# Weight loads, fp8 rounding and side jobs in other slots of an attention loop, and two head columns centred on VectorE

## What is computed

```python
x = x + tanh(g_xattn) * xattn(layernorm(x), ctx)     # 8 groups of heads
x = x + tanh(g_ffn) * ffn(layernorm(x))
# xattn
ln = ln(hidden) ; q = fp8_linear(ln, wq); k = fp8_linear(ln, wk); v = ...; qx = fp8_linear(ln, wqx)
kx, vx = split(einsum(cond, w_kv_x));   q, k, qx, kx are layer-normed per head of 128
core = gqa(q, k, v); xout = gqa(qx, kx, vx)          # softmax(q k^T / sqrt(d)) v
out = einsum(fp8(cat(core, xout) / smooth), wproj) * scales
# fp8_linear: fp8(clip(x / in_scale, -448, 448)) * in_scale, times wq, times a scale
# ffn: bitlinear(x, w): x rounded to int8 steps per token; w -> clip(round(w / mean|w|), -1, 1) * mean|w|
```

## Time and profile before

| | us |
|---|---|
| median of three runs | 1812.07 (1807.82 to 1817.33) |
| the profiled execution | 1815.84 |
| its span, first to last instruction | 1814.1 |
| preamble and ramp, up to the first exponential (slot 0) | 115.6 |
| slots 0 to 511 | 1372.1 |
| the tail behind them | 326 |

### The profile page before, as it was taken

One profiled execution on the slowest core, in us unless ns is written; L12 is line 12 of the kernel. 1 busy time (PEld: TensorE's weight loads), 2 busy tenths in 40 slices (PEclk: granted clock), 3 DMA queues, 4 the chain that ended last, 5 costly groups with the idle time before them and its releaser, 6 DMA issues.

```text
span 1814.1 us, 35237 instructions
## 1 busy us (share of the span) xinstructions
PE 1620.1 (89%) x11164; PEld 1005.9 (55%) x11164; DVE 1533.6 (85%) x3391; ACT 1371.8 (76%) x3439; POOL 1100.2 (61%) x1421
## 2 busy tenths in 40 slices
PE   2368899889999999999999898999999978999997
PEld 1345555555666665666566555666666633444443
DVE  7568889999897899989887999999988876777776
ACT  6458999879989998999998788899988872222222
POOL 3677888877887777787776666777767641000000
PEclk9689999999999999999999999999999999999999
DMA  3257888779999998999897989999998896243200
GB/s 104 90 151 164 186 194 190 178 169 230 230 244 196 218 226 191 205 217 250 193 216 169 224 192 200 222 229 225 251 222 169 184 246 216 70 112 87 76 24 18
DMA packets 669596, 325.48 MB, mean 179 GB/s; under 512 B 552288, under 2 KB 595424, under 8 KB 669152
## 3 DMA queue, kind: packets, MB, share of 16 engines
q1 hardware_dynamic: 669408, 323.17, 79.2%
HBM read 140.61 MB, written 48.23 MB: 104 GB/s over the span
## 4 chain that ended last, share of the span: by engine, by line
PE 45%; DVE 24%; ACT 12%; issue 8%; POOL 7%; DMA 4%; SPq 0%; ACTq 0%; POOLq 0%; DVEq 0%
PE psum L699 8%; PE psum L654 8%; PE psum L687 7%; PE psum L742 6%; PE psum L717 6%; DVE pp L987 5%; DVE nmx L977 5%; PE psum L661 3%; PE psum L760 3%; ACT pp L1334 2%; DMA pt<-pp 2%; ACT psum L1323 2%; PE psum L674 2%; ACT raw L1254 2%; DVE xh L960 1%
## 5 line engine op out<-in xcount | busy, mean ns | idle before, releaser
L687 PE MATMUL psum<-qk 128*128 128x512 f16 x1536 | 422.5, 384 | 21.6 <-DVE pp L987 15.8
L699 PE MATMUL psum<-pt,vv 128*128 128x512 f16 x1536 | 399.3, 383 | 37.2 <-ACT cy L1342 22.4
L654 PE MATMUL psum<-wbt,xqt 128*128 128x256 f16 (+1 forms) x4096 | 408.7, 249 | 22.1 <-DVE xqt L904 11.4
L1323 ACT ACTIVATE psum<-psum,nmx 128x512 f32<-128x512 f32 x512 | 352.4, 688 | 69.6 <-DVE nmx L977 68.0
L654 PEld LDWEIGHTS psum<-wbt,xqt 128*128 128x128 f16 x4096 | 329.5, 99 | 136.2 <-issue 18.4
L987 DVE SCALAR_TENSOR_TENSOR pp<-psum,prs,pp 128x512 f16<-128x512 f32 x512 | 378.7, 740 | 3.3 <-ACT pp L1334 3.3
L1334 ACT ACTIVATE pp<-psum,prs 128x512 f16<-128x512 f32 x512 | 366.0, 715 | 6.2 <-DMA pt<-pp 5.9
L977 DVE TENSOR_REDUCE nmx<-psum 128x1 f32<-128x512 f32 x512 | 344.8, 674 | 28.6 <-PE psum L687 28.0
L699 PEld LDWEIGHTS psum<-pt,vv 128*128 128x128 f16 x1536 | 147.5, 98 | 234.5 <-issue 54.2
L1579 POOL TENSOR_TENSOR qk<-y,qk 128x512 f16<-128x512 f32 x192 | 231.8, 1207 | 16.0
L687 PEld LDWEIGHTS psum<-qk 128*128 128x128 f16 x1536 | 143.8, 99 | 105.4 <-DVE pp L987 24.8
(11 more groups left out here) (176 smaller groups left out, 2792.3 us busy)
## 6 DMA issues: line engine op xcount, KB each, us to landing
wbt<-ws SPq DMA_DIRECT2D x192, 256.0 KB, 3.7
ws<-wbt SPq DMA_DIRECT2D x64, 256.0 KB, 4.1
catd<-cy SPq DMA_DIRECT2D x64, 256.0 KB, 3.2
raw<-in_wgu SPq DMA_DIRECT2D x64, 256.0 KB, 3.6
raw<-in_w SPq DMA_DIRECT2D x32, 384.0 KB, 3.9
wbt<-catd SPq DMA_DIRECT2D x6, 2048.0 KB, 9.8
pt<-pp SPq DMA_TRANSPOSE x512, 3.8
raw<-in_wp SPq DMA_DIRECT2D x32, 256.0 KB, 3.6
```

Of the source, the lines that this page charges most:

```text
L654: ins = e.matmul(bank[:, o0:o0 + c1 - c0], xv[:, v, kt * 512 + tt * 128:kt * 512 + (tt + 1) * 128], wb[i][:, h, kt, c0:c1], start=kt == 0 ...
L687: ins = e.matmul(SB(n), qk[i][:, jq, u, ss], qk[i][:, jk, w, :], start=k == 0, stop=k == 2)
L699: ins = e.matmul(OB, v[:, t, u, att, :], src[:, w, t, :], start=t == 0 and k == 0, stop=t == 3 and k == 2)
L1323: e.activation(SB(n), SB(n), ACT.Exp, bias=nmx[:, k], accum_out=psm[:, k]).then_inc(s["exp"], 1)
```

## The change

1. **Weight loads.** The load slots of groups 1 to 3 move later: group 1's tiles 3, 4, 5 from -20, -20, -19 to -16, -14, -13; group 2's from (-8, -4, -3, -1, -13, -12) to (-4, 0, 1, 2, -8, -7); group 3's from (8, 12, 13, 15, 3, 4) to (9, 12, 13, 15, 5, 6). Every step that follows a load moves with it.
2. **Activation rounding.** The 40 steps run at 28 + floor(1.9 k) instead of 62 + k, and take the first half of all four v, then the second half.
3. **Jobs.** All 48 sums come first with eight splits (slots 92 to 231, one every 2.5 slots), the reduction in slots 218, 228 and 229, then 20 ternary jobs (236 to 287), 24 splits mixed with four ternary jobs (288 to 361), and the last 24 ternary jobs (362 to 441, one every 3.3 slots). The flag's reduction moves to 366, 372, 373; the first reload of the gate weight from 444 to 448.
4. **Centring.** From group 2 on VectorE centres and scales the first two head columns of each tile in one instruction on 128x256 elements, in the slot of "near", and ScalarE's "near" does column 2 only. `w_hi` on GpSimd also waits for it (`w_ce`).

```diff
-RAMP_LOAD = (-27, -26, -25, -20, -20, -19)
+RAMP_LOAD = (-27, -26, -25, -16, -14, -13)
+FIRST_LOADS = {1: RAMP_LOAD, 2: (-4, 0, 1, 2, -8, -7), 3: (9, 12, 13, 15, 5, 6)}
...
-PREP = {"mean": 2, "near": 3, "far": 4, "hi": 5, "lo": 6}
+PREP = {"mean": 2, "centre": 3, "near": 3, "far": 4, "hi": 5, "lo": 6}
...
+DVE_MID = 2
+WG_AT, CAT_AT, X2_AT = (448, 490), (474, 498), 507
...
+SCALE_AT = {"sum": 218, "whole": 228, "fac": 229}
+FLAG_AT = {"sum": 366, "whole": 372, "fac": 373}
...
-    "quant": tuple(range(62, 102)),
+    "quant": tuple(28 + k * 19 // 10 for k in range(40)),
...
+    return FIRST_LOADS[it][t] if it in FIRST_LOADS else (it - 2) * SLOTS + TILE_LOAD[t]
...
-JOBS = [t for i in range(16) for t in SUMS[3 * i:3 * i + 3] + SPLITS[2 * i:2 * i + 2]]
-JOBS += [("scale", None, 0, 0)]
-JOBS += [("tern", "wgu", j, j) for j in range(32)] + [("tern", "wd", j, 32 + j) for j in range(16)]
+TERNS = [("tern", "wgu", j, j) for j in range(32)] + [("tern", "wd", j, 32 + j) for j in range(16)]
+JOBS = SUMS + SPLITS[:8] + [("scale", None, 0, 0)] + TERNS[:20]
+JOBS += [t for i in range(4) for t in SPLITS[8 + 6 * i:14 + 6 * i] + TERNS[20 + i:21 + i]] + TERNS[24:]
+
+JOB_SPANS = ((92, 231, 56), (232, 233, 1), (236, 288, 20), (288, 362, 28), (362, 442, 24))
...
+            def head_centre(it, t):
+
+                k = place_of(it, t)
+                q.wait_ge("wm", k + 1)
+                r = raw[k % 3][:, 0:256].rearrange("p (k n) -> p k n", k=2)
+                e.scalar_tensor_tensor(r, r, ratio[:, t, 0:1], wmean[:, k % 3, 0:2].unsqueeze(2).broadcast_to([128, 2, 128]),
+                                       ALU.mult, ALU.add).then_inc(s["w_ce"], 1)
...
-                v, half_ = divmod(part, 2)
+                half_, v = divmod(part, 4)
...
-                    q.wait_ge("xy", xy_value(b, 3, v))
+                    q.wait_ge("xy", xy_value(b, 2 * half_ + 1, v))
...
+                for it, kt in prep_at(n, "centre"):
+                    if it >= DVE_MID:
+                        head_centre(it, kt)
...
-                    w_mid(it, kt, 0, 3)
+                    w_mid(it, kt, 2 if it >= DVE_MID else 0, 3)
...
+                q.wait_ge("w_ce", (it - DVE_MID) * 4 + kt + 1)
                 q.wait_ge("wc", k + 1)
```

More of the change, by code:

```diff
@@ L46 @@
 ACT_NORM = 2 * 4
-WG_AT, CAT_AT, X2_AT = (444, 490), (474, 498), 507
+DVE_MID = 2
+WG_AT, CAT_AT, X2_AT = (448, 490), (474, 498), 507
 RAMP = -4
 OUT_AT = {"clip": 17, "field": 18, "step": 19, "add": 20, "sub": (21, 23), "store": 26}
-JOBS_FROM, TERN_FROM = 92, 309
-SCALE_AT = {"sum": 303, "whole": 308, "fac": 309}
-FLAG_AT = {"sum": 306, "whole": 324, "fac": 325}
+JOBS_FROM = 92
+SCALE_AT = {"sum": 218, "whole": 228, "fac": 229}
+FLAG_AT = {"sum": 366, "whole": 372, "fac": 373}
 X_AT = {
@@ L95, in load_slot @@
 def load_slot(it, t):
-    return RAMP_LOAD[t] if it == 1 else (it - 2) * SLOTS + TILE_LOAD[t]
+    return FIRST_LOADS[it][t] if it in FIRST_LOADS else (it - 2) * SLOTS + TILE_LOAD[t]
 def tiles_of(n, after):
@@ L154, in job_slots @@
 def job_slots():
-    scale = JOBS.index(("scale", None, 0, 0))
-    at = {JOBS_FROM + m * 8 // 3: m for m in range(scale)}
-    at.update({TERN_FROM + (m - scale) * 8 // 3: m for m in range(scale, len(JOBS))})
+    at, m = {}, 0
+    for first, last, count in JOB_SPANS:
+        at.update({first + k * (last - first) // count: m + k for k in range(count)})
+        m += count
     at[JOBS_FROM - 4] = -1
@@ L242, in xq_value @@
 def xq_value(b, v):
-    return v + 1 if b == 0 else 4 + 8 * (b - 1) + 2 * v + 2
+    return v + 1 if b == 0 else 4 + 8 * (b - 1) + 4 + v + 1
 class Queue:
@@ L268 @@
     "pre_v pre_p pre_a pre_h pre_r pre_f pre_w const_ready x_mv x_rs x_n x_tr xy x_w x_q "
-    "cx_pt cxp cxs cxw cxf cx_md cx_hi cx_lo wxp wxs wxw wxf wx_pt wm wc w_hi w_dn gf "
+    "cx_pt cxp cxs cxw cxf cx_md cx_hi cx_lo wxp wxs wxw wxf wx_pt wm w_ce wc w_hi w_dn gf "
     "ga gb vh vx_lo a_st b_st a_rs b_rs a_n b_n b_na hd_tr y32 hd_hi hd_lo "
@@ L1010, in job @@
                 q.wait_ge("l_t1", JV["l_t1", m])
-                q.wait_ge(f"l_st{i}", JV[f"l_st{i}", stored])
-                q.wait_ge("l_ab", JV["l_ab", summed])
+                if stored is not None:
+                    q.wait_ge(f"l_st{i}", JV[f"l_st{i}", stored])
+                if summed is not None:
+                    q.wait_ge("l_ab", JV["l_ab", summed])
                 q.done(e.tensor_scalar(ob, f, MAGIC, 1.0, ALU.subtract, ALU.min))
```

## The result

| | before | after |
|---|---|---|
| median, us | 1814.38 (1807.56 to 1820.2) | 1818.88 (1810.28 to 1822.06) |
| runs | 20 | 20 |
| ratio | | 1.0027, 95% interval 1.0016 to 1.0037 |
| span of the profiled execution | 1814.1 | 1818.8 |
| mean granted TensorE clock | 0.976 | 0.964 |

The change makes the kernel slower by 0.27%, some 4.5 us, less than the 0.5% that counts as a difference here. The forecast was 1783.8, and its range ended at 1806.

What follows compares the result with a forecast made beforehand. TensorE sets a floor of about 39 us per sixteen slots; fuller VectorE or ScalarE cost time above it. First batch -2.9, second -3.6, third -16.8, loads -5 sum to -28.3: 1783.8 against the median, range 1757 to 1806.

Steps and rivals of the forecast that it cites:

- The ramp's gain: Before slot 0: moving loads later regains 10 of TensorE's 20.8 us of waiting, bounds 0 and 20.8.
- The ring: Slots 0 to 15: three raw buffers get tight, VectorE waits up to 3.1 us at four places; 5 of 12.4 taken.
- the ring takes the gain back and more: Rival, chance 0.15: nothing gained before slot 0, four full stalls of 3.1 us, -10.9 in all, 1801.2.
- The centring's price: VectorE, 24 tiles from group 2: 0.6 us each, 2.4 per stretch, bounds 0.33 and 1.12.
- the flat 0.5 per rounding step: VectorE: every rounding step costs 0.5 us, as derived from slots 336 to 351.
- the idle time that was added to the fullest engine: Each stretch: new busy time of its fullest engine plus the idle time such stretches show, 0.1 to 0.8 us where VectorE alone is full.
- The three stretches of the sum: Second batch: slots 192 to 207 -2.9, 208 to 223 -2.5, 240 to 255 +1.8, together -3.6 us.
- the stretches taken as nil: Stretches not named in the sum change by one or two jobs and were counted as 0.
- the rule from busy time to stretch: Stretches of sixteen slots: fullest engine's busy time plus idle time; with a third engine as near, 42 us.
- The move of the scale matmul: From slot 308 to slot 228, without a transpose of x near; slot 308, 5.7 us before, falls under 3.
- The port: Rival, chance 0.05: VectorE waits for GpSimd, up to +35 us at 120 rounding steps and +12 at 24 centrings, 1831.
- The better balance: Rival, chance 0.12: slots 288 to 351 come down to 39.7, first batch stays at 48, ramp's 10 stay whole: 1764.

Runs made afterwards that it cites:

- e8: Kernel before with the jobs' new order, the moved rounding and a fourth raw buffer, loads and centring as before: 1792.05 us, ratio 0.9885.
- e10: Kernel before with new jobs and rounding, four raw buffers, group 1's loads late, group 2's tiles 1 to 3 in slots -2, -1, 0, no centring: 1794.29 us, 0.9904.
- e5: Changed kernel with four raw buffers and group 2's tiles 1 to 3 loaded in slots -2, -1 and 0: 1805.63 us, ratio 0.9954 to before.
- e1: Changed kernel with the weight loads alone put back in their old slots: 1807.81 us, ratio 0.9962 to before.
- e12: Kernel before with the later weight loads and nothing else: 1825.21 us, ratio 1.0076.
- e3: Changed kernel with the weight loads and the centring both undone, so only jobs and rounding are new: 1798.36 us, ratio 0.9911 to before.
- e11: Kernel with mended loads and four raw buffers, two ternary jobs and one split alternating from slot 236 to 441: 1793.29 us, ratio 0.9902 to before.
- e6: Kernel before with the moved rounding steps alone: 1806.49 us, ratio 0.9945.
- e9: Kernel before with the centring on VectorE alone: 1818.44 us, ratio 1.002.

## Why the prediction was wrong, point by point

**Ramp and slots 0 to 15: -5 forecast, +12.6 measured.** The ramp's gain was taken as 10 and is 4.5. In the kernel after TensorE still stands 13.2 us for `w_spread`, for the 20.8 of the earlier trace rows, and 8.6 us in the ramp for GpSimd's tiles of keys and values (0.3 before), which now come late themselves. With the fourth buffer and group 2 earlier slot 0 comes at 104.4, near the 105 of the prediction, but not by its step: the buffer alone gives 108.3 (e8), so the moved loads bring 2.5 to 3.9 there (e10, e5), and 3.1 to 5.4 with three buffers (e1, e12). The ring was foreseen, with its places and a price of up to 12.4, of which it took 5, since it could overlap with idle time. The failed steps, beside that size, are three. The price counted VectorE's stalls (14.0 measured, so 12.4 was near) and not the transposes that queue behind the same wait on SyncE, though the sentence named them: they cost TensorE 4.8. It did not count the second mechanism at all, the margin of group 2's last tile, cut from four slots to one: 6.9. And it had no term for TensorE's longer busy time at the clock of 0.85, 2.8. The rival "the ring takes the gain back and more" had the mechanism, but its price, four stalls of 3.1, ended at 1801.2.

**Slots 16 to 95: -2.9 forecast, +5.5 measured.** The forecast said that part 4 gains in slots 16 to 31 and costs about as much behind. It costs 8 to 10 us in all by the medians, some 5 of it in these slots. The centring's price was nearly right: 0.6 taken, 0.64 by its records' mean over the 24, and 0.75 by VectorE's busy time (1541.5 to 1559.6). VectorE's busy time over the five stretches is right in sum, 239.2 for 238.0, though not in place: slots 32 to 47 have 51.1 for 49.1 and 64 to 79 have 52.3 for 50.1, slots 48 to 63 have 46.7 for 49.2. Behind the places stands the flat 0.5 per rounding step. In e3, without centring, the eight steps of slots 32 to 47 make VectorE 5.2 busier (42.66 to 47.83), 0.65 each, and the centring lengthens them once more.

The larger part of the 8.4 is the failed step: the idle time that was added to the fullest engine. It was 7.5 us over the five stretches in the forecast and is 14.7. Slots 16 to 31 show it alone: VectorE 46.1 and ScalarE 45.2 busy, as forecast (45.8, 44.9), and 50.1 us for 47.8. In slots 32 to 47 it is 3.1 for 0.7, where the clock was 0.91; in e1, at a clock of 1.00, VectorE's 51.5 gave 51.9. Why slots 16 to 31, with two engines near each other, take 4.0 us more than the fuller of them isn't shown.

The Trainium skill, SBUF — State Buffer, section "SBUF: two separate sides", says that a VectorE instruction with two SBUF inputs and GpSimd hold the port pair for a whole instruction each, and that the later one waits. The trace agrees in direction: the ten long records began beside a large GpSimd instruction and ended behind one, and of the short ones only the one at 123.05 began inside one. It differs in two things: GpSimd's small instructions lengthened none, and the long ones end 0.27 us behind the large one, less than the 0.47 that a centring takes alone.

**Second batch: -3.6 forecast, -3.7 measured.** The three stretches of the sum held within 1 us: slots 192 to 207 took 40.4 for 41.2, slots 208 to 223 took 43.8 for 43.0, slots 240 to 255 took 39.2 for 40.2. They add to -4.6; the stretches taken as nil add +1.0, so that the total agrees to a tenth of a microsecond is luck.

**Third batch: -16.8 forecast, -8.2 measured.** The busy times came out within 2 us of those forecast: in slots 320 to 335 VectorE 41.2 (39.4 forecast) and ScalarE 38.5 (39.8), in slots 336 to 351 VectorE 40.0 (38.3) and ScalarE 40.3 (41.0). The failed step is again the rule from busy time to stretch: with three engines near 40 it was put at 42, and they took 45.1 and 44.4, 5.5 of the 8.6 missed. Slots 288 to 303 took 44.1 for 42.2 with ScalarE at 41.7 (41.4 forecast), 1.9 more, and slots 272 to 287 and 368 to 383, taken as nil, 0.9 and 0.5. Slots 304 to 319 (42.1 for 43.2) and 352 to 367 (42.2 for 41.6) held. That lower maxima of the sums don't cure it is what e11 suggests: it lowers some, raises others and gains nothing. What in the slots makes up the 3 to 4 us above the fullest engine, perhaps the order of pieces within a slot, stays open. The move of the scale matmul did what it says: slot 308 takes 3.5 us in place of 5.7 (under 3 was forecast), and slot 228, where it is now, 2.9, as before.

**The rivals.** The port was given 0.05, with its price at the 120 rounding steps and the 24 centrings. It showed at both, in a smaller size. The 120 steps take 77.4 us by their records before, 85.3 in e3 and 87.3 in the kernel after, 10 more for the 35 that the rival had, and in e6 they still gain (0.9945). In the kernel after 46 of them are over 15% longer than the shortest of their kind, and all 46 began inside a GpSimd instruction of 0.55 us or more; before there were 31, of which 30 began so. Not every step that begins so is lengthened: 31 weren't. The argument against the rival, that the bunched steps cost 0.5 beside a GpSimd just as busy, misread its row: in slots 336 to 351 GpSimd is busy for 31.3 of 47.5 us, in slots 32 to 47 for 41.4 of 47.7. The better balance didn't come. The change does what it says in all four parts; two of them cost, 11 us for the loads and 8 for the centring, and two gain 16.

**What stays open.** Alone, the parts give -16 (parts 2 and 3), +14 (part 1) and +4 (part 4), some +1 in all, and the whole gave +4.9. The intervals of these are up to 5 us either way, so the difference isn't shown to be more than noise. If it is more, the meeting of centring and rounding on VectorE is the likely place (+4 in e9, +9 from e3 to e1, -0.4 and +4.9 us in slots 16 to 95).
